# Attention block on one core: P.V of all sixteen heads in one block, in slot 3 of the following step

## The chip, the core and the metric

The kernel runs on one NeuronCore of a Trainium2 chip. Five engines work side by side, each through its own instruction stream in order: TensorE (PE, matrix products and transposes, results in PSUM), VectorE (DVE), ScalarE (ACT), GpSimd (POOL) and SyncE (SP, which issues most DMAs). They wait for one another through semaphores. The metric is the device time of one execution in microseconds; lower is better.

## What is computed

For each of sixteen batch elements of 256 tokens by 256 features: a layer norm scaled and shifted by a condition vector, sixteen-head attention with heads of 16 features, a projection, the residual sum and the same norm again.

```python
h = _sln(hidden, w, ln_g, ln_b, Wg, bg, Wb, bb)
qkv = (h @ Wqkv.T + bqkv).reshape(B, N, num_heads, hd, 3)
energy = jnp.einsum('bhqd,bhkd->bhqk', q, k)
att = jax.nn.softmax(energy, axis=-1) / D ** 0.5
out = jnp.einsum('bhqk,bhkd->bhqd', att, v)
out = jnp.moveaxis(out, 1, 2).reshape(B, N, D)
out = out @ Wp.T + bp
h1 = out + hidden
h2 = _sln(h1, w, ln_g, ln_b, Wg, bg, Wb, bb)
return h2 + h1
```

B = 16, N = D = 256, sixteen heads, everything float32.

## The kernel before

The program is a pipeline over batch elements. `step(b)`, written once for each engine, runs over sixteen **slots** h = 0 to 15, one for each head; after steps -1 to 14 a last step is written out by hand. Different batch elements are in different stages of one step:

- **Scores.** In slot h PE computes `scores(b, h)` into the banks `st` (two matmuls, keys by queries), and ACT turns them into exponentials `p32[:, h]` (L585). Banks `st0` and `st1` alternate, so scores of slot h wait for the exponential of slot h-2.
- **Maxima.** In the same slot PE computes `scores_max(b + 1, h)`, queries by keys, into the banks `sa` (two matmuls); DVE takes the row maxima `mx` from them (L664, `maximum`). These banks alternate too: `scores_max` of slot h waits for the maximum of slot h-2. After eight heads PE transposes the maxima (`transpose_max`, slots 1 and 9), ACT writes `m_h` and DVE `m_l` (`low_max`), which POOL sends by DMA into rows of the stacked queries, so that the exponentials need no subtraction.
- **Projections.** Q and K of b+2, V of b+1 and the output projection of b-1 come in quarters of three matmuls, in the slots that `Q_SLOTS`, `K_SLOTS`, `V_SLOTS` and `P_SLOTS` list.
- **P.V.** `weigh(b, g)` multiplies the exponentials of eight heads by V: 16 matmul instructions (32 rows of the trace), four of them side by side in column groups of 32, into bank `pv_ps[g]`. `PV_SLOTS = (10, 2)`: the first eight heads in slot 10 of step b, the other eight in slot 2 of step b+1. ACT copies a bank to `oT` (`evict_out`, L534), PE transposes it back (`out_by_token`, four transposes, L1034), DVE divides by the sums (`normalise`: `rec`, then `att`).
- **After both halves** PE transposes `att` (`turn_att`, slot 10, L1115), ACT copies the result to `aT_h` (L559), DVE subtracts for `aT_l` (`low_att`, L749), and the output projection takes both from slot 12 on. The quarter in slot 12 waits for `aT_l`.
- **The next input.** `turn_x(b + 3)` (four transposes) in slot 10, then `hT` and `hT_h` on ACT.

What DVE does between the maxima is the dictionary `between` of its `step`: (h, 0) stands before the maximum of slot h, (h, 1) behind it. `residual(b - 2, 0..5)` is the residual sum, its statistics and the two passes that write `y`; `norm1(b + 3, 0..2)` the statistics of the next input; `low_qk` the low parts of Q and K. Each engine keeps to its written order: an instruction that waits holds all that stands behind it on that engine.

Of the kernel before, what the change touches and what calls it, by code (L numbers as in the profile page):

```python
# [32 lines left out]
P = 128  # L33
B, N, D, H = 16, 256, 256, 16
HD = D // H
KT = D // P
# [17 lines left out]
S_O1, S_O0 = 3, 12  # L54
S_OT1, S_OT0 = 6, 14


def cond_block(nc, x, condT, vectors, WgT, WbT, WqkvT, WpT, bp, out):
    gb_dram = nc.dram_tensor("gb_rows", (B, 2 * D), F32, kind="Internal").ap()
    with ExitStack() as ctx:  # L60
# [10 lines left out]
        wqkv = sb("wqkv", [P, KT, 3 * D])  # L71
# [5 lines left out]
        wg = sb("wg", [P, KT, D])  # L77
# [36 lines left out]
        p32 = sb("p32", [P, H, KT * N])  # L114
# [138 lines left out]
        def max_sent(a, g):  # L253

            return 32 * (half(a) + (1 if g or par(a) else 0)) if a >= 0 else 0

# [223 lines left out]
        def _(act):  # L480
# [55 lines left out]
            def step(b):  # L536
                for h in range(H):
                    if h == S_O1:
                        evict_out(b - 1, 1)
                    if h == S_O0:  # L540
# [96 lines left out]
            for h in range(H):  # L637
                wait(act, st_done, 16 * (B - 1) + h + 1)
                if h % HH == 0:
                    wait(act, pv_done, 2 * (B - 2) + h // HH + 1)  # L640
                nc.scalar.activation(p32[:, h, :], last_st[h % 4][:], ACT.Exp).then_inc(exp_done, 1)
                if h == 1:
                    high_max(B - 1, 1, pv_ps[0])
# [12 lines left out]
        def _(dve):  # L656
# [169 lines left out]
            def step(b):  # L826


                between = {
                    (2, 1): [lambda: low_max(b, 1)],  # L830
                    (3, 0): [lambda: residual(b - 2, 0), lambda: residual(b - 2, 1)],
                    (4, 0): [lambda: residual(b - 2, 2), lambda: norm1(b + 3, 0)],
                    (4, 1): [lambda: residual(b - 2, 3), lambda: norm1(b + 3, 1)],
                    (5, 0): [lambda: norm1(b + 3, 2)],
                    (5, 1): [lambda: low_qk(b + 2, 0, m0, qh_ready, ql_ready)],
                    (7, 0): [lambda: normalise(b - 1, 1, 0)],
                    (7, 1): [lambda: low_qk(b + 2, 1, m1, kh_ready, kl_ready)],
                    (8, 0): [lambda: normalise(b - 1, 1, 1)],
                    (9, 1): [lambda: residual(b - 2, 4)],
                    (11, 0): [lambda: low_max(b + 1, 0), lambda: low_att(b - 1), lambda: residual(b - 2, 5)],  # L840
                    (15, 0): [lambda: normalise(b, 0, 0)],
                    (15, 1): [lambda: normalise(b, 0, 1)],
                }
                if first(b + 1):
                    for slot in ((4, 0), (4, 1), (5, 0), (5, 1), (7, 1), (11, 0)):
                        del between[slot]
# [96 lines left out]
        def _(pe):  # L943
# [63 lines left out]
            def weigh(b, g):  # L1007
# [11 lines left out]
                for q in range(2):  # L1019
                    for k in range(TT):  # L1020
                        for j in range(4):
                            h = HH * g + 4 * q + j
                            o = mm(pv_ps[g][32 * j:32 * j + VC, q * N:(q + 1) * N], v_st[:, p, k, h, :],
                                   p32[:, h, k * N:(k + 1) * N], k == 0, k == TT - 1)
# [110 lines left out]
            def last_weigh(half):  # L1135
# [7 lines left out]
                for k in range(TT):  # L1143
                    for j in range(4):
                        h = HH + 4 * half + j
                        o = mm(bank[32 * j:32 * j + VC, 0:N], v_st[:, p, k, h, :],
                               p32[:, h, k * N:(k + 1) * N], k == 0, k == TT - 1)
# [75 lines left out]
            def step(b):  # L1223
                for h in range(H):
# [11 lines left out]
                    for g in range(2):  # L1236
                        a = b - g
                        if h == PV_SLOTS[g] and has(a):
                            weigh(a, g)
                    if h == S_OT1:  # L1240
                        out_by_token(b - 1, 1)
                    if h == S_OT0:
                        out_by_token(b, 0)
                    if h == S_MT1 and has(b):
                        wait(pe, att_ready, 2 * (b - 1) + 1)
# [106 lines left out]
```

## Time and profile before

| | |
|---|---|
| median of 3 runs | 352.46 us (350.66 to 354.25) |
| the profiled execution, whole | 353.58 us |
| its span in the profile | 351.8 us |
| busy share of the span | PE 96%, DVE 85%, ACT 69%, POOL 45% |
| chain of work that ended last, by engine | PE 87%, DVE 5%, DMA 2% |
| clock granted to PE | 0.995 of full speed on average |

The profiled execution spent 1.8 us outside its span, and is 1.1 us above the median of the runs. In the rows below, a start to start distance is the time that an instruction holds its place in an engine's stream; the duration printed beside it reaches beyond that, since both matmuls and DVE operations overlap with the one behind.

### The profile page before, as it was taken

What the parts mean: (1) busy time and instruction counts of PE and PEld (TensorE: products, weight loads), DVE (VectorE), ACT (ScalarE), POOL (GpSimd) and SP (SyncE); (2) the same over time, 40 slices, a digit from 0 to 9 for tenths busy, and PEclk for the clock granted to TensorE, in tenths of its full rate; (3) what the DMA queues carried; (4) which work ended last, traced back from release to release, by engine and by line L of the source; (5) the groups of instructions that cost most, each with busy time, mean ns of one, the idle gap of its engine ahead of it and who ended that gap; (6) DMA issues with size and microseconds to landing.
All of it is one profiled execution on the core that took longest, in us unless ns stands there. A gap on an engine that the chain in (4) does not pass through costs nothing.

```text
span 351.8 us, 8975 instructions
## 1 busy us (share of the span) xinstructions
PE 336.8 (96%) x3170; PEld 290.8 (83%) x3171; DVE 299.9 (85%) x732; ACT 241.8 (69%) x472; POOL 156.7 (45%) x185
## 2 busy tenths in 40 slices
PE   7978899999999999999999999999999999999974
PEld 4757868889898888888898988888898988888753
DVE  4679677789898999989898989989898988998773
ACT  7643687767778686868678686868686786666730
POOL 5382271535464462726454553717354643234330
PEclk9999899999999999999999999999999999999999
DMA  8297344544546465555455455654556453642031
GB/s 240 73 229 195 84 122 123 154 132 125 169 133 158 137 179 154 146 160 144 138 154 158 134 159 150 171 161 133 164 140 157 103 159 104 174 124 63 4 89 60
DMA packets 47705, 48.87 MB, mean 139 GB/s; under 512 B 6287, under 2 KB 41374, under 8 KB 47662
## 3 DMA queue, kind: packets, MB, share of 16 engines
q1 hardware_dynamic: 44494, 46.74, 48.4%
q10 hardware_dynamic: 1184, 1.07, 1.1%
q0 software_dynamic: 1984, 0.51, 0.8%
q8 instruction: 25, 0.41, 0.5%
q14 instruction: 18, 0.15, 0.1%
HBM read 9.99 MB, written 4.23 MB: 40 GB/s over the span
## 4 chain that ended last, share of the span: by engine, by line
PE 87%; DVE 5%; DMA 2%; ACT 1%; issue 1%; ACTq 1%; POOL 0%; SPq 0%; DVEq 0%
PE m L945 25%; PE st L945 18%; PE sa L945 18%; PE pv L945 17%; PE pv L1034 4%; DVE mx L664 2%; PE pv L1115 2%; PE m L1074 2%; DMA kst<-qk_l 1%; DMA vrows<-vectors_dram 1%; DVE qk_l L699 1%; PE pv L1048 1%; ACTq L608 1%; DVE y L780 1%; PE m L1048 1%
## 5 line engine op out<-in xcount | busy, mean ns | idle before, releaser
L664 DVE TENSOR_REDUCE mx<-sa 128x2 f32<-128x512 f32 x256 | 171.8, 684 | 31.7 <-PE sa L945 30.7
L585 ACT ACTIVATE p<-st 128x512 f32<-128x512 f32 x240 | 141.0, 598 | 39.0 <-PE st L945 34.7
L945 PE MATMUL sa<-kst,qst 126*128 126x256 f32 x512 | 106.0, 289 | 3.1 <-DVE mx L664 2.0
L945 PE MATMUL st<-qst,kst 128*128 128x256 f32 x496 | 104.8, 294 | 0.5 <-DMA qst<-m_l 0.3
L945 PEld LDWEIGHTS st<-qst,kst 128*128 128x128 f32 x496 | 75.8, 190 | 14.2 <-issue 12.8
L945 PEld LDWEIGHTS sa<-kst,qst 126*128 126x128 f32 x512 | 79.2, 191 | 5.7 <-DVE mx L664 2.4
L365 POOL DMA_DIRECT2D qst<-m_h x31 | 17.6, 567 | 114.0 <-DVE m_l L673 114.0
L945 PE MATMUL pv<-p,v_st 128*32 128x256 f32 x1008 | 61.0, 382 | 0.0
L945 PEld LDWEIGHTS pv<-p,v_st 128*32 128x32 f32 x1008 | 29.5, 109 | 21.0 <-issue 1.4
L945 PE MATMUL m<-hT_h,wqkv_h 128*128 128x256 f32 x128 | 38.0, 311 | 1.6 <-POOL hT_l L406 0.9
L374 POOL TENSOR_SCALAR xn<-xa,mv,rstd 128x256 f32<-128x256 f32 x28 | 34.2, 1227 | 1.5
L945 PE MATMUL m<-hT_l,wqkv_h 128*128 128x256 f32 x128 | 34.5, 281 | 0.0
L945 PE MATMUL m<-hT_h,wqkv_l 128*128 128x256 f32 x128 | 34.5, 281 | 0.0
L420 POOL TENSOR_TENSOR rstd<-vare,minus_half 128x4 f32<-128x4 f32 (+1 forms) x16 | 14.9, 932 | 40.0 <-DVE vare L721 36.0
L534 ACT ACTIVATE oT<-pv 128x512 f32<-128x512 f32 x29 | 17.2, 594 | 21.6 <-PE pv L945 21.6
L699 DVE SCALAR_TENSOR_TENSOR qk_l<-m,vecs,qk_h 128x256 fp32r<-128x256 f32 x64 | 27.7, 475 | 1.1 <-ACT qk_h L506 1.0
L945 PEld LDWEIGHTS m<-hT_h,wqkv_h 128*128 128x128 f32 x128 | 24.4, 199 | 2.8 <-issue 1.7
L945 PEld LDWEIGHTS m<-hT_h,wqkv_l 128*128 128x128 f32 x128 | 23.8, 191 | 0.0
L945 PEld LDWEIGHTS m<-hT_l,wqkv_h 128*128 128x128 f32 x128 | 23.7, 191 | 0.0
L392 POOL TENSOR_TENSOR h1b<-h,gb 128x512 f32<-128x512 f32 x15 | 19.3, 1285 | 9.7 <-DMA gb<-gb_rows 9.7
L406 POOL TENSOR_TENSOR hT_l<-hT,hT_h 128x512 fp32r<-128x512 f32 x14 | 18.0, 1288 | 10.5 <-ACT hT_h L487 10.5
L383 POOL TENSOR_TENSOR xa<-xa,bias_b 128x512 f32<-128x512 f32 x16 | 20.6, 1291 | 0.0
(147 smaller groups left out, 566.0 us busy)
## 6 DMA issues: line engine op xcount, KB each, us to landing
qst<-qk_h SPq DMA_DIRECT2D x64, 128.0 KB, 2.4
qst<-qk_l SPq DMA_DIRECT2D x64, 128.0 KB, 2.5
kst<-qk_h SPq DMA_DIRECT2D x62, 128.0 KB, 2.5
kst<-qk_l SPq DMA_DIRECT2D x62, 128.0 KB, 2.7
xa<-x_dram SPq DMA_DIRECT2D x16, 256.0 KB, 3.0
gb<-gb_rows SPq DMA_DIRECT2D x16, 256.0 KB, 3.8
out_dram<-y SPq DMA_DIRECT2D x15, 256.0 KB, 2.2
wqkv<-WqkvT_dram SPq DMA_DIRECT2D x1, 512.0 KB, 5.6
```

The costliest lines, as they stand in the source:

```text
L365: pool.dma_start(raw(qst[MAX_ROW + r:MAX_ROW + 1 + r, p, g * HH:(g + 1) * HH, :]) .rearrange("a h (t n) -> a (h t) n", t=TT), raw(m[:, g, ...
L374: o = pool.tensor_scalar(xn[:, t, :], xbuf(a)[:, t, :], mv[:, t, 0:1], rstd[:, 0, t:t + 1], ALU.subtract, ALU.mult)
L383: pool.tensor_tensor(xbuf(a), xbuf(a), bias_b[:].rearrange("p (a n) -> p a n", a=1).broadcast_to([P, TT, D]), ALU.add).then_inc(xdb_ready, 1)
L392: pool.tensor_tensor(h1b[:], h1[:], gb[:, par(a), D:2 * D].rearrange("p (a n) -> p a n", a=1) .broadcast_to([P, TT, D]), ALU.add).then_inc ...
L406: pool.tensor_tensor(hT_l[:, par(a)], hT[:], hT_h[:, par(a)], ALU.subtract).then_inc(hTl_ready, 1)
L420: pool.tensor_tensor(rstd[:, which], vare[:, which], minus_half[:, which], ALU.pow).then_inc(rstd_ready, 1)
L534: nc.scalar.activation(oT[:, g, :], pv_ps[g][:], ACT.Copy).then_inc(oT_ready, 1)
L585: nc.scalar.activation(p32[:, h, :], st_ps[h % 2][:], ACT.Exp).then_inc(exp_done, 1)
L664: dve.tensor_reduce(mx[:, par(a), h // HH, (h % HH) * TT:(h % HH + 1) * TT], sa_ps[h % 2][:].rearrange("p (t n) -> p t n", t=TT), AX.X, AL ...
L699: o = dve.scalar_tensor_tensor(out=qk_l[:, par(a), t, g, :], in0=ps[:, g * N:(g + 1) * N], scalar=vecs[:, 4 + t, g:g + 1], in1=qk_h[:, par ...
L945: return nc.tensor.matmul(o, l, r, start=start, stop=stop)
L1034: o = nc.tensor.transpose(pv_ps[g][:, t * N + c * P:t * N + (c + 1) * P], oT[:, g, c * N + t * P:c * N + (t + 1) * P], ident[:])
```

## The change

Both calls of `weigh` for one batch element now stand behind one another in slot 3 of the following step. For that the exponentials of a whole step have to outlive it, so `p32` becomes a ring of twenty heads instead of sixteen (the weights `wqkv` and `wg`, which only the start reads, are laid into its last four). The two copies to `oT` stand together in slot 4 on ACT, the two `out_by_token` in slots 4 and 5 on PE, and `normalise` in slots 5 to 7 on DVE. Nearly all the work that DVE did between the maxima of slots 3 to 5 moves to one place before the maximum of slot 4. Some projection quarters shift by a slot or two; `turn_x` moves from slot 10 to 11, the copy of V on ACT from 9 to 10. Steps 1 to 14 have the joined block; in step 14 the first half of element 14 stays in slot 10, and the last step keeps its order.

```diff
-PV_SLOTS = (10, 2)
-
-Q_SLOTS, K_SLOTS, V_SLOTS, P_SLOTS = (0, 1, 3, 4), (4, 5, 5, 6), (7, 7, 8, 8), (12, 13, 14, 15)
-S_MT1, S_AT, S_MT0, S_XT = 1, 10, 9, 10
-S_QH, S_KH, S_VH = 5, 7, 9
+PV_SLOT, PV_LAST = 3, 10
+RING = 20
+
+Q_SLOTS, K_SLOTS, V_SLOTS, P_SLOTS = (0, 1, 1, 2), (4, 5, 6, 6), (7, 8, 8, 9), (12, 13, 14, 15)
+S_MT1, S_AT, S_MT0, S_XT = 1, 10, 9, 11
+S_QH, S_KH, S_VH = 4, 7, 10
...
-S_O1, S_O0 = 3, 12
-S_OT1, S_OT0 = 6, 14
+S_OUT, S_O0 = 4, 12
+S_OT, S_OT0 = (4, 5), 14
...
-        p32 = sb("p32", [P, H, KT * N])
+        p32 = sb("p32", [P, RING, KT * N])
...
+                    if h == S_OUT:
+                        evict_out(b - 1, 0)
+                        evict_out(b - 1, 1)
...
-                        if h % HH == 0:
+                        if h % HH == RING - H:
                             wait(act, pv_done, 2 * (b - 1) + h // HH + 1)
-                        nc.scalar.activation(p32[:, h, :], st_ps[h % 2][:], ACT.Exp).then_inc(exp_done, 1)
+                        nc.scalar.activation(p32[:, ring(b, h), :], st_ps[h % 2][:], ACT.Exp).then_inc(exp_done, 1)
...
-                    wait(pe, ml_ready, 2 * b + 2)
+                    wait(pe, ml_ready, 2 * (b + 1 if b < B - 2 else b) + 2)
...
-                    for g in range(2):
-                        a = b - g
-                        if h == PV_SLOTS[g] and has(a):
-                            weigh(a, g)
-                    if h == S_OT1:
-                        out_by_token(b - 1, 1)
-                    if h == S_OT0:
+                    if h == PV_SLOT and has(b - 1):
+                        weigh(b - 1, 0)
+                        weigh(b - 1, 1)
+                    if h in S_OT:
+                        out_by_token(b - 1, S_OT.index(h))
+                    if h == PV_LAST and b == B - 2:
+                        weigh(b, 0)
+                    if h == S_OT0 and b == B - 2:
                         out_by_token(b, 0)
```

Where the order changes most, in a step of the middle. On PE, slots 10 to 12 before (`xn` is the next input, `att` the attention output by token, `wp` the output projection's weights):

```order
L945 MATMUL sa<-kst,qst 128x256 [waits max_done]
L945 MATMUL sa<-kst,qst 128x256
L1074 MATMUL m<-ident,xn 128x128 [waits xn_ready,v_ready]
L1074 MATMUL m<-ident,xn 128x128 x3
L1115 MATMUL pv<-ident,att 128x128 [waits att_ready]
L1115 MATMUL pv<-ident,att 128x128 x3
L945 MATMUL pv<-p,v_st 32x256 [waits v_ready,ml_ready,att_ready,exp_done]
L945 MATMUL pv<-p,v_st 32x256 x15
L945 MATMUL st<-qst,kst 128x256 [waits exp_done]
```

The same place on PE in the changed kernel, from the transposes of `att` to the first quarter of the output projection:

```order
L1121 MATMUL pv<-ident,att 128x128 [waits att_ready]
L1121 MATMUL pv<-ident,att 128x128 x3
L951 MATMUL st<-qst,kst 128x256 [waits exp_done]
L951 MATMUL st<-qst,kst 128x256
L951 MATMUL sa<-kst,qst 128x256 [waits max_done]
L951 MATMUL sa<-kst,qst 128x256
L1080 MATMUL m<-ident,xn 128x128 [waits xn_ready,v_ready]
L1080 MATMUL m<-ident,xn 128x128 x3
L951 MATMUL st<-qst,kst 128x256 [waits exp_done]
L951 MATMUL st<-qst,kst 128x256
L951 MATMUL sa<-kst,qst 128x256 [waits max_done]
L951 MATMUL sa<-kst,qst 128x256
```

The block of P.V has gone from between the transposes of `att` and the pairs behind them; the transposes of `xn` stand there instead, one slot later than before. On PE, the new place of the block, from the maxima's pair of slot 3 to the scores of slot 4:

```order
L951 MATMUL sa<-kst,qst 128x256 [waits max_done]
L951 MATMUL sa<-kst,qst 128x256
L951 MATMUL pv<-p,v_st 32x256 [waits v_ready,ml_ready,att_ready,exp_done]
L951 MATMUL pv<-p,v_st 32x256 x15
L951 MATMUL pv<-p,v_st 32x256 [waits aTl_ready,att_ready,exp_done]
L951 MATMUL pv<-p,v_st 32x256 x15
L951 MATMUL st<-qst,kst 128x256 [waits exp_done]
```

Its first matmul waits for `ml_ready`, the `m_l` of the maxima that were transposed in slot 1 of the same step; the block that stood in slot 2 before did not. On DVE, around slot 11 in the changed kernel, where the list is as it was before (`y` is the output, `aT_l` feeds the output projection):

```order
L786 SCALAR_TENSOR_TENSOR y<-h,mv,gb 128x256 [waits gb_in0,y_out0]
L786 SCALAR_TENSOR_TENSOR y<-h,mv,gb 128x256
L670 TENSOR_REDUCE mx<-sa 128x2 [waits mT_done,sa_done]
L679 SCALAR_TENSOR_TENSOR m_l<-m,m_h 16x128 [waits mh_ready]
L755 TENSOR_TENSOR aT_l<-pv,aT_h 128x512 [waits aTh_ready]
L794 SCALAR_TENSOR_TENSOR y<-y,rstd,h1b 128x256 [waits h1b_ready,rstd_ready,ln2_step]
L794 SCALAR_TENSOR_TENSOR y<-y,rstd,h1b 128x256
L670 TENSOR_REDUCE mx<-sa 128x2 [waits mT_done,sa_done] x8
```

These rows keep their order and their places between the maxima; what PE does beside them is different.

## Rows read from the trace of the kernel before

**Rows 1.** Timeline of PE: first scores of steps 2 and 12 (start and duration in us)
```profile
73.75 0.28 PE L945 MATMUL st<-qst,kst 128*128 128x256 f32 x1
...
268.73 0.28 PE L945 MATMUL st<-qst,kst 128*128 128x256 f32 x1
```
**Rows 2.** Busy time in step 6: stretch, length, PE, PEld, DVE, ACT, POOL; clock
```profile
151.75:171.24 19.49, 19.49 (x196) 17.29 (x195) 17.84 (x45) 14.57 (x30) 9.37 (x10) 1.00 0.52 151
```
**Rows 3.** Timeline of PE around the block in slot 2 of step 7
```profile
172.54 0.28 PE L1048 MATMUL pv<-ident,mx 128*128 128x128 f32 x1
...
173.24 0.40 PE L945 MATMUL sa<-kst,qst 126*128 126x256 f32 x2
173.56 1.93 PE L945 MATMUL pv<-p,v_st 128*32 128x256 f32 x32
175.43 0.51 PE L945 MATMUL st<-qst,kst 128*128 128x256 f32 x2
175.77 0.40 PE L945 MATMUL sa<-kst,qst 126*128 126x256 f32 x2
176.01 0.28 PE L945 MATMUL m<-hT_h,wqkv_h 128*128 128x256 f32 x1
```
**Rows 4.** The same for slots 10 to 13 of step 6
```profile
163.69 0.51 PE L945 MATMUL sa<-kst,qst 126*128 126x256 f32 x2
164.03 0.60 PE L1074 MATMUL m<-ident,xn 128*128 128x128 f32 x4
164.47 0.60 PE L1115 MATMUL pv<-ident,att 128*128 128x128 f32 x4
165.00 1.93 PE L945 MATMUL pv<-p,v_st 128*32 128x256 f32 x32
...
167.92 0.28 PE L945 MATMUL m<-wp_h,aT_h 128*128 128x256 f32 x1
...
168.27 0.39 PE L945 MATMUL st<-qst,kst 128*128 128x256 f32 x2
...
168.74 0.28 PE L945 MATMUL m<-wp_h,aT_h 128*128 128x256 f32 x1
```
**Rows 5.** The same, a narrow window: the last four matmuls of that block
```profile
166.54 0.40 PE L945 MATMUL pv<-p,v_st 128*32 128x256 f32 x4
```
**Rows 6.** Timeline of DVE, slots 7 to 11 of step 6 (in brackets: idle before)
```profile
161.85 0.86 DVE L699 SCALAR_TENSOR_TENSOR qk_l<-m,vecs,qk_h 128x256 fp32r<-128x256 f32 x2
162.62 0.41 DVE L687 TENSOR_TENSOR att<-pv,rec 128x256 f32<-128x256 f32 x1
162.96 1.28 DVE L664 TENSOR_REDUCE mx<-sa 128x2 f32<-128x512 f32 x2
164.15 0.87 DVE L780 SCALAR_TENSOR_TENSOR y<-h,mv,gb 128x256 f32<-128x256 f32 x2
164.94 0.68 DVE L664 TENSOR_REDUCE mx<-sa 128x2 f32<-128x512 f32 x1
165.54 0.27 DVE L673 SCALAR_TENSOR_TENSOR m_l<-m,m_h 16x128 fp32r<-16x128 f32 x1
165.74 0.69 DVE L749 TENSOR_TENSOR aT_l<-pv,aT_h 128x512 fp32r<-128x512 f32 x1
166.35 0.87 DVE L788 SCALAR_TENSOR_TENSOR y<-y,rstd,h1b 128x256 f32<-128x256 f32 x2
167.65 0.69 DVE L664 TENSOR_REDUCE mx<-sa 128x2 f32<-128x512 f32 x1 [0.42 <-PE sa L945]
```
**Rows 7.** Timeline of DVE, slot 2 of step 7
```profile
173.67 0.69 DVE L664 TENSOR_REDUCE mx<-sa 128x2 f32<-128x512 f32 x1 [0.24 <-PE sa L945]
```
**Rows 8.** Timeline of ACT, slot 11 of step 6
```profile
165.11 0.60 ACT L559 ACTIVATE aT_h<-pv 128x512 fp32r<-128x512 f32 x1 [0.34 <-PE pv L1115]
165.60 1.02 ACT L568 ACTIVATE hT<-m,bfull,gfull 128x256 f32<-128x256 f32 x2
166.65 0.63 ACT L487 ACTIVATE hT_h<-hT 128x512 fp32r<-128x512 f32 x1
```

More of the change, by code:

```diff
@@ L76, in cond_block @@
         wp_l = sb("wp_l", [P, KT, D], F32R)
-        wg = sb("wg", [P, KT, D])
         wb = sb("wb", [P, KT, D])
@@ L113, in cond_block @@
         m_l = sb("m_l", [HH * TT, 2, P], F32R)
-        p32 = sb("p32", [P, H, KT * N])
+        p32 = sb("p32", [P, RING, KT * N])
+        wqkv = p32[:, H:H + 3, :].rearrange("p a n -> p (a n)").rearrange("p (k n) -> p k n", k=KT)
+        wg = p32[:, H + 3, :].rearrange("p (k n) -> p k n", k=KT)
         oT = sb("oT", [P, 2, 2 * N])
@@ L255, in max_sent, with ring @@
             return 32 * (half(a) + (1 if g or par(a) else 0)) if a >= 0 else 0
+        def ring(a, h):
+            return (H * a + h) % RING
         def xbuf(a):
@@ L537, in step @@
                 for h in range(H):
-                    if h == S_O1:
-                        evict_out(b - 1, 1)
-                    if h == S_O0:
+                    if h == S_O0 and b == B - 2:
                         evict_out(b, 0)
@@ L638, in _ @@
                 wait(act, st_done, 16 * (B - 1) + h + 1)
-                if h % HH == 0:
+                if h % HH == RING - H:
                     wait(act, pv_done, 2 * (B - 2) + h // HH + 1)
-                nc.scalar.activation(p32[:, h, :], last_st[h % 4][:], ACT.Exp).then_inc(exp_done, 1)
+                nc.scalar.activation(p32[:, ring(B - 1, h), :], last_st[h % 4][:], ACT.Exp).then_inc(exp_done, 1)
                 if h == 1:
@@ L830, in step @@
                     (2, 1): [lambda: low_max(b, 1)],
[L831 to L836, printed above, removed]
+                    (4, 0): [lambda: residual(b - 2, 0), lambda: residual(b - 2, 1), lambda: residual(b - 2, 2),
+                             lambda: norm1(b + 3, 0), lambda: residual(b - 2, 3), lambda: norm1(b + 3, 1),
+                             lambda: norm1(b + 3, 2), lambda: low_qk(b + 2, 0, m0, qh_ready, ql_ready)],
+                    (5, 0): [lambda: normalise(b - 1, 0, 0)],
+                    (5, 1): [lambda: normalise(b - 1, 0, 1)],
+                    (6, 0): [lambda: normalise(b - 1, 1, 0)],
+                    (7, 0): [lambda: normalise(b - 1, 1, 1)],
                     (7, 1): [lambda: low_qk(b + 2, 1, m1, kh_ready, kl_ready)],
-                    (8, 0): [lambda: normalise(b - 1, 1, 1)],
                     (9, 1): [lambda: residual(b - 2, 4)],
                     (11, 0): [lambda: low_max(b + 1, 0), lambda: low_att(b - 1), lambda: residual(b - 2, 5)],
-                    (15, 0): [lambda: normalise(b, 0, 0)],
-                    (15, 1): [lambda: normalise(b, 0, 1)],
-                }
+                }
+                if b == B - 2:
+                    between[(15, 0)] = [lambda: normalise(b, 0, 0)]
+                    between[(15, 1)] = [lambda: normalise(b, 0, 1)]
                 if first(b + 1):
-                    for slot in ((4, 0), (4, 1), (5, 0), (5, 1), (7, 1), (11, 0)):
-                        del between[slot]
+                    between = {}
                     between[(2, 0)] = [lambda: low_qk(1, 0, m0, qh_ready, ql_ready)]
@@ L1023, in weigh @@
                             o = mm(pv_ps[g][32 * j:32 * j + VC, q * N:(q + 1) * N], v_st[:, p, k, h, :],
-                                   p32[:, h, k * N:(k + 1) * N], k == 0, k == TT - 1)
+                                   p32[:, ring(b, h), k * N:(k + 1) * N], k == 0, k == TT - 1)
                 o.then_inc(pv_done, 1)
@@ L1146, in last_weigh @@
                         o = mm(bank[32 * j:32 * j + VC, 0:N], v_st[:, p, k, h, :],
-                               p32[:, h, k * N:(k + 1) * N], k == 0, k == TT - 1)
+                               p32[:, ring(B - 1, h), k * N:(k + 1) * N], k == 0, k == TT - 1)
                 o.then_inc(pvt_done, 1)
@@ L1235, in step @@
                         turn_att(b - 1)
-                    for g in range(2):
-                        a = b - g
-                        if h == PV_SLOTS[g] and has(a):
-                            weigh(a, g)
-                    if h == S_OT1:
-                        out_by_token(b - 1, 1)
-                    if h == S_OT0:
+                    if h == PV_SLOT and has(b - 1):
[6 more added lines that the diff above has]
+                    if h == S_OT0 and b == B - 2:
                         out_by_token(b, 0)
                     if h == S_MT1 and has(b):
-                        wait(pe, att_ready, 2 * (b - 1) + 1)
+                        wait(pe, att_ready, 2 * (b - 2) + 1)
                         if first(b):
```

1 line of the change is left out of this document (removed).

## The prediction

> **What bounds the kernel now.** I read first how regular the steps are, then which engine is busy all through one, then the rows around the two blocks. The first scores of steps 2 and 12 start at 73.75 and 268.73 [rows 1], ten steps apart, so one step is 19.50 us. In such a step PE is busy for 19.49 of 19.49 us and DVE for 17.84 [rows 2]: PE sets the pace, and DVE has only 1.65 us to spare. Its places between the maxima matter, because PE computes maxima for two heads at most ahead of DVE. That limit shows already in one place: the maxima of slot 10 start at 163.69, just after the maximum of slot 8 ended (162.96 + 0.68 = 163.64), and hold PE for 0.34 instead of 0.24 us [rows 4, 6]. So a semaphore from DVE takes 0.05 us to reach PE, and a wait costs 0.10 us beyond its length.
>
> What keeps DVE from holding PE up elsewhere is the block in slot 10. DVE's group at slot 11 (`m_l`, `aT_l` and the second pass of `y`, ending 0.79 after 166.35) fits beside PE's block from 165.00 to 166.87, and DVE then even waits 0.42 us for the next maxima [rows 4, 6]. The same block covers the way from the transposes of `att` over `aT_h` and `aT_l` to the output projection's first quarter: `aT_l` ends at 166.43, and the quarter starts at 167.92 [rows 4, 6].
>
> **What the change saves on PE.** Going into the block costs 0.08 us (the pair before it holds 0.32 instead of 0.24), leaving it 0.10 (0.34 instead of 0.24), and the block itself holds 1.87 us [rows 3]. Inside, eight groups of four matmuls start from 165.00 to 166.54 [rows 4, 5], 1.54 / 7 = 0.22 us apart, so eight more groups in the same block cost about 1.75, not 1.87. One block fewer saves 0.08 + 0.10 + 0.12 = 0.30 us a step. The wait of slot 10 goes too, another 0.10: in the count further down the maximum of slot 8 ends at 0.43 + 0.60 + 0.77 + 0.69 = 2.49, and PE comes to slot 10's maxima at 2.93. Were there no other wait, a step would take 19.50 - 0.40 = 19.10 us.
>
> The Trainium skill says in TensorEngine Tiling (Array Packing), Key Properties, that changing the tiling mode drains TensorE, and P.V is the only work here in columns of 32. The trace agrees: it shows the 0.08 and 0.10 us above. By this rule alone the change gains, and that is the first rival below.
>
> **What it costs in slot 3.** The block's first matmul now waits for `m_l` of maxima transposed in slot 1. Counted from that transpose: it takes 0.11 (172.54 to 173.24 is 0.70, less a quarter, 0.35, and half a pair, 0.24 [rows 3, 4]); then two quarters (0.70), the pair of slot 2 (0.47), a quarter (0.35), the pair of slot 3 (0.47) and the way in (0.08) bring PE to 2.18. The pair is 168.27 to 168.74, the quarter 167.92 to 168.27 [rows 4]. DVE must first take the maximum of slot 2. Those maxima start at 0.11 + 0.70 + 0.24 = 1.05 on PE; the maximum follows 0.43 later (173.24 to 173.67 [rows 3, 7]), at 1.48; `m_l` follows 0.60 behind it and lasts 0.27 [rows 6], to 2.35; PE sees it at 2.40. That is a wait of 0.22 us, with everything behind it on PE held.
>
> DVE's long list before the maximum of slot 4 costs nothing: it lies in a stretch in which PE, busy with P.V for 3.6 us, delivers no maxima. The copies to `oT` also stand beside the block: the first half is copied during the second, and the second while PE does slot 4.
>
> **What it costs in slots 11 to 13.** The list at slot 11 stays, but the block beside it is gone. I count from the start of slot 7's maxima on PE. Ahead of slot 13's maxima PE has: the rest of that pair 0.24 and a quarter 0.35; slot 8, pair and two quarters, 1.17; slot 9, pair, transpose, quarter, 0.93; slots 10 and 11, a pair and four transposes each (0.47 + 0.44, the latter 164.03 to 164.47 [rows 4]), 1.82; slot 12, pair and quarter, 0.82; half a pair 0.24. Sum 5.57 us.
>
> DVE in the same stretch, by start to start distances [rows 6]: 0.43 to the maximum of slot 7, which takes 0.60; low part of K 0.77; maxima of slots 8 and 9 1.19; first pass of `y` 0.79; maximum of slot 10 0.60; `m_l` 0.20; `aT_l` 0.61; second pass of `y` 0.79; maximum of slot 11 in full 0.69. With the semaphore's 0.05 that is 6.72. All these stand in this order, and none waits for PE by more than 0.03, since PE is ahead. So slot 13's maxima come 6.72 - 5.57 = 1.15 us late, plus 0.10. About 0.34 of it shows earlier, at the output projection's first quarter: `aT_l` ends at 0.43 + 0.60 + 0.77 + 1.19 + 0.79 + 0.60 + 0.20 + 0.69 = 5.27, and PE sees it at 5.32; PE is there at 5.57 - 0.35 - 0.24 = 4.98.
>
> DVE cannot make this up ahead of slot 7: its lag there starts from zero, as it waits for PE's maxima after the block (the pairs of slots 4 to 7 are 1.2 us or so apart, a maximum takes 0.60).
>
> A step then takes 19.10 + 0.22 + 1.15 + 0.10 = 20.57 us, 1.07 more than before.
>
> **Is ScalarE any help?** No, it would hold PE at almost the same place. From the transposes of `att` (164.47) to the copy `aT_h` (165.11) 0.64; the copy 0.49; an exponential taken as the same 0.49; `hT` 1.05 (165.60 to 166.65); `hT_h` at least 0.5, then the exponential of slot 12, 0.6 [rows 4, 8]: 3.8 us. PE waits for it at the scores of slot 14, which it would reach 0.44 + 0.91 + 0.82 + 0.82 = 2.99 after those transposes. So even if DVE were fast, PE would lose about 0.8 us there. In step 1, which has no `y` on DVE, this takes DVE's place.
>
> **The ends.** Step 0 loses its block and four transposes: 1.87 + 0.18 + 0.44 = 2.5 at most, nothing at least; ScalarE's group is then uncovered there too, and I take 1.3. Steps 1 to 12: 12 x 1.07 = 12.8. Step 13 has no `turn_x`, so PE was 0.44 faster there and is now held to DVE's time all the same: 1.07 + 0.44 = 1.5. Step 14 takes the half that step 0 lost without its own way in, 1.75, and the wait of slot 3, more with no Q quarters ahead of it, 0.4: 2.1. The last step is as before. Sum: -1.3 + 12.8 + 1.5 + 2.1 = 15.1 us. The profiled execution, on which this rests, took 353.58; it would become 368.7. It was 1.1 us above the median, so against 352.46 I expect 367.5 us.
>
> **Rivals.**
> - *The saving alone.* By the rule of the drain: 13 steps x -0.40, step 0 -1.3, step 14 +1.75, in all -4.8: 347.7 us. It speaks for it that DVE has 1.65 us to spare over a step, against it that the spare time lies in the wrong slots: it decides if slot 11's list were done 1.15 us sooner than the rows add up to. 4%.
> - *Only the chains, not the list.* If just the wait of slot 3 (0.22) and of the output projection (0.34 + 0.10) stayed, a step would be 19.76, 0.26 more: 13 x 0.26 - 1.3 + 2.1 = +4.2, 356.6, and with the shortest of both waits within 1%. Against it stands that `y` is written ahead of slot 11's maximum. 5%.
> - *More waits than I count.* Queries and keys for the next maxima are sent by SP when slot 7's scores and the low part of K are done; if their landing held the next step's slot 0 by another 0.5 us, 13 x 0.5 brings 374. DVE's chain moves the step's end back as well, which gives them room. 6%.
> - The forecast: 85%.
>
> **How the numbers follow.** A measurement of this kernel tells about 1% from no change, 348.9 to 356.0. The range must hold errors of the count: half of the loss of slots 11 to 13 would give 367.5 - 13 x 0.55 = 360.3; another 0.4 us a step 372.7. So 360.5 to 373, which leaves out the first two rivals and the top of the third. Faster 0.04; same 0.04 (the lower part of the second rival, the upper of the first); slower 0.92.
>
> **What would show it right or wrong.** In the profile after, a step of 20.5 to 20.6 us; one block of 3.6 us a step; PE idle or late before the block in slot 3 (0.2, for `m_l`), at the output projection's first quarter (0.3, for `aT_l`), and before slot 13's maxima (0.8, for the maximum of slot 11); DVE without idle time from slot 7 to slot 12, and idle after the block instead. Wrong would be a step under 19.5, DVE with idle time between slots 8 and 11, or a wait at the start of slot 0.

## The result, and the profile after

The changed kernel takes 368.24 us (median of 4 runs, 367.39 to 370.46) where the kernel before took 352.57 (4 runs, 350.66 to 354.25): a ratio of 1.046, 95% interval 1.041 to 1.051. The forecast was 367.5, range 360.5 to 373. The profiled execution took 367.54 us, with a span of 365.7.

In that profile PE is busy for 92% of the span (96% before), DVE for 84% (85%), ACT for 65% (69%).

The timeline of PE gives the first scores of steps 2 and 12 (start and duration), which answers [rows 1]:

```profile
71.45 0.28 PE L951 MATMUL st<-qst,kst 128*128 128x256 f32 x1
...
276.87 0.28 PE L951 MATMUL st<-qst,kst 128*128 128x256 f32 x1
```

The windows view of step 6 answers [rows 2] (stretch, length, busy time and count of PE, PEld, DVE, ACT, POOL; granted clock):

```profile
153.61:174.15 20.54, 19.59 (x197) 17.76 (x195) 18.38 (x45) 14.43 (x30) 9.35 (x11) 1.00 0.53 145
```

Ten steps in 205.42 us: a step is 20.54 us instead of 19.50. PE was busy all through a step before; now 0.95 us of each step is idle. PE does the same matmuls, so the loss is waiting. The timeline of PE in step 6 shows where (start, duration, line, operation, count; in brackets the idle time before, and what ended it). First slot 3, then slots 12 and 13:

```profile
156.77 0.40 PE L951 MATMUL sa<-kst,qst 126*128 126x256 f32 x2
157.41 3.66 PE L951 MATMUL pv<-p,v_st 128*32 128x256 f32 x64 [0.24 <-DVE m_l L679]
161.00 0.51 PE L951 MATMUL st<-qst,kst 128*128 128x256 f32 x2
...
169.85 0.41 PE L951 MATMUL sa<-kst,qst 126*128 126x256 f32 x2
170.43 0.39 PE L951 MATMUL m<-wp_h,aT_h 128*128 128x256 f32 x1 [0.17 <-DVE aT_l L755]
...
170.89 0.39 PE L951 MATMUL st<-qst,kst 128*128 128x256 f32 x2
171.82 0.50 PE L951 MATMUL sa<-kst,qst 126*128 126x256 f32 x2 [0.54 <-DVE mx L670]
172.16 0.28 PE L951 MATMUL m<-wp_h,aT_h 128*128 128x256 f32 x1
```

Three places are held, all by DVE. The idle time in brackets is less than what is lost, because a modelled matmul end covers part of it; starts tell the loss. The pair before the block holds 0.64 us (156.77 to 157.41) instead of the 0.32 of [rows 3]: 0.32 lost. The pair before the output projection's first quarter holds 0.58 instead of 0.24, and the quarter itself 0.46 (170.43 to 170.89) instead of the 0.35 of [rows 4]: 0.45 lost. The scores of slot 13 hold 0.93 (170.89 to 171.82) and the maxima behind them 0.34, each instead of 0.24: 0.79 lost. In all 1.56 us, and 20.54 - 1.56 = 18.98 us is the step without waits. The block itself holds 3.59 us.

The other side is the timeline of DVE in the same step, which answers [rows 6 and 7]:

```profile
156.38 0.69 DVE L670 TENSOR_REDUCE mx<-sa 128x2 f32<-128x512 f32 x1 [0.59 <-PE sa L951]
156.99 0.27 DVE L679 SCALAR_TENSOR_TENSOR m_l<-pv,m_h 16x128 fp32r<-16x128 f32 x1
...
165.51 0.69 DVE L670 TENSOR_REDUCE mx<-sa 128x2 f32<-128x512 f32 x1 [0.17 <-PE sa L951]
166.12 0.86 DVE L705 SCALAR_TENSOR_TENSOR qk_l<-m,vecs,qk_h 128x256 fp32r<-128x256 f32 x2
166.91 1.29 DVE L670 TENSOR_REDUCE mx<-sa 128x2 f32<-128x512 f32 x2
168.12 0.87 DVE L786 SCALAR_TENSOR_TENSOR y<-h,mv,gb 128x256 f32<-128x256 f32 x2
168.91 0.68 DVE L670 TENSOR_REDUCE mx<-sa 128x2 f32<-128x512 f32 x1
169.51 0.27 DVE L679 SCALAR_TENSOR_TENSOR m_l<-m,m_h 16x128 fp32r<-16x128 f32 x1
169.70 0.67 DVE L755 TENSOR_TENSOR aT_l<-pv,aT_h 128x512 fp32r<-128x512 f32 x1
170.30 0.86 DVE L794 SCALAR_TENSOR_TENSOR y<-y,rstd,h1b 128x256 f32<-128x256 f32 x2
```

`m_l` ends at 157.26, and the block's first group of matmuls starts at 157.41. From 165.51 on no row has idle time ahead of it: DVE works its list through, and PE, which had the block to do beside it before, stands behind it. In [rows 6] DVE was the one that waited after the second pass of `y`, for 0.42 us.

ScalarE's group around slot 12, from its timeline, answers [rows 8] (`aT_h` starts at 168.94, ahead of these rows):

```profile
169.90 1.05 ACT L574 ACTIVATE hT<-m,bfull,gfull 128x256 f32<-128x256 f32 x2
170.98 0.63 ACT L492 ACTIVATE hT_h<-hT 128x512 fp32r<-128x512 f32 x1
171.51 1.07 ACT L591 ACTIVATE p<-st 128x512 f32<-128x512 f32 x2
```

The exponential of slot 12 starts only at 171.51, yet PE shows no wait for ScalarE: in slot 13 it waits for DVE until 171.82 anyway. Over the whole run the waits view lists (us in total, times, longest):

```profile
...
PE sa L951 <- DVE mx L670: 9.9, 18, 1.2
...
PE pv L951 <- DVE m_l L679: 3.7, 14, 0.5
...
PE m L951 <- DVE aT_l L755: 2.2, 12, 0.3
```

The times of the first scores of every step in both traces give the whole difference of the spans, in us:

| stretch | before | after | difference | forecast |
|---|---|---|---|---|
| to the first scores of step 0 | 35.59 | 33.09 | -2.5 | 0 |
| step 0 | 18.67 | 17.28 | -1.4 | -1.3 |
| step 1 | 19.49 | 21.08 | +1.6 | +1.07 |
| steps 2 to 11 | 10 x 19.50 | 10 x 20.54 | +10.4 | +10.7 |
| step 12 | 19.50 | 20.79 | +1.3 | +1.07 |
| step 13 | 19.03 | 20.69 | +1.7 | +1.5 |
| step 14 | 17.07 | 19.37 | +2.3 | +2.1 |
| last step | 27.44 | 28.02 | +0.6 | 0 |
| sum | 351.77 | 365.73 | +14.0 | +15.1 |

### The profile page after: what moved, and what is told of

Read it like the earlier page. It is cut to its first block, busy times and chain, and to the rows that moved or that the text cites. A ratio compares the mean times of both kernels' runs of the same rounds, so it can differ in the third digit from the quotient of the medians.

```text
span 365.7 us, 8975 instructions
## 1 busy us (share of the span) xinstructions
PE 335.7 (92%) x3171; PEld 294.7 (81%) x3171; DVE 306.8 (84%) x732; ACT 239.4 (65%) x472; POOL 157.8 (43%) x185
## 3 DMA queue, kind: packets, MB, share of 16 engines
q10 hardware_dynamic: 1184, 1.07, 1.1%
## 4 chain that ended last, share of the span: by engine, by line
PE 60%; DVE 21%; issue 10%; ACT 4%; DMA 2%; ACTq 1%; POOL 1%; DVEq 0%
PE pv L951 16%; PE m L951 15%; PE sa L951 12%; PE st L951 11%; DVE mx L670 9%; PE pv L1040 4%; DVE y L786 3%; DVE qk_l L705 3%; DVE y L794 2%; DVE m_l L679 1%; ACT qst L595 1%; DMA kst<-qk_l 1%; DMA qst<-m_l 1%; ACT p L591 1%; ACT hT L574 1%
## 5 line engine op out<-in xcount | busy, mean ns | idle before, releaser
L951 PE MATMUL st<-qst,kst 128*128 128x256 f32 x496 | 103.2, 290 | 2.2 <-ACT p L591 2.1
L951 PEld LDWEIGHTS sa<-kst,qst 126*128 126x128 f32 x512 | 78.3, 189 | 15.9 <-DVE mx L670 12.7
L951 PE MATMUL pv<-p,v_st 128*32 128x256 f32 x1008 | 58.1, 380 | 3.7 <-DVE m_l L679 3.7
L951 PEld LDWEIGHTS pv<-p,v_st 128*32 128x32 f32 x1008 | 36.6, 110 | 20.0 <-issue 5.6
L951 PEld LDWEIGHTS m<-hT_h,wqkv_h 128*128 128x128 f32 x128 | 23.5, 189 | 3.5 <-issue 1.2
L411 POOL TENSOR_TENSOR hT_l<-hT,hT_h 128x512 fp32r<-128x512 f32 x14 | 17.9, 1280 | 15.1 <-ACT hT_h L492 15.1
L951 PE MATMUL m<-wp_h,aT_h 128*128 128x256 f32 x64 | 20.0, 313 | 2.3 <-DVE aT_l L755 2.2
```

The costliest lines, as they stand in the source:

```text
L411: pool.tensor_tensor(hT_l[:, par(a)], hT[:], hT_h[:, par(a)], ALU.subtract).then_inc(hTl_ready, 1)
L951: return nc.tensor.matmul(o, l, r, start=start, stop=stop)
```

## The experiments

A step below is the distance from one step's first scores to the next's, in the steps of the middle of the profiled execution. "Beside" gives the kernel before on the same chip. The theory is that of the prediction: three holds by DVE and, hidden behind them, one by ScalarE. The rivals are that PE itself is slower with the joined block, or that one hold alone carries the loss and the others only move.

**The wait for `m_l` alone.** `m_l` is written before the maximum of slot 2 instead of after it:

```diff
-                    (2, 1): [lambda: low_max(b, 1)],
+                    (2, 0): [lambda: low_max(b, 1)],
```

> The changed kernel, with m_l of the second eight heads made before the maximum of slot 2 instead of behind it; nothing else. A step of the changed kernel takes 20.54 us, and the block in slot 3 starts 0.24 us late for m_l. If that wait is a loss of its own, as the prediction counted it, it goes and a step takes 20.25 to 20.35 us, with the waits in slots 12 and 13 as they were. If the joined block starves VectorE (the rival theory: the idle time behind the block is the loss), an earlier block changes nothing: 20.5 us.

Measured: a step of 20.25 us, 0.29 less than 20.54; the run took 364.83 us, beside 351.13. The wait before the block is gone, and those of slots 12 and 13 are as they were (idle 0.17 and 0.53). So the hold of slot 3 is a loss of its own, and what is given back there isn't taken again further on.

**ScalarE's group alone.** One half of `hT` is written in slot 12, the other in slot 13, `hT_h` in slot 14 (in short):

```diff
-                        for k in range(KT):
+                        for k in range(KT if first(b + 1) else 1):
...
+                    if h == S_XT + 2 and not first(b + 1) and has(b + 3):
+                        nc.scalar.activation(hT[:, 1, :], ...).then_inc(hT_ready, 1)
-                    if h == (X_FIRST if first(b + 1) else S_XT) + 1:
+                    if h == (X_FIRST + 1 if first(b + 1) else S_XT + 3):
                         high_h(b + 3)
```

> The changed kernel, with ScalarE's hT of the next input spread over slots 12 and 13 and hT_h moved to slot 14, so that its exponentials of slots 12 to 14 come sooner; VectorE as it was. The theory of the prediction: VectorE's list still holds PE, 20.5 to 20.6 us a step. If ScalarE's group were the holder: about 20.0 us.

Measured: 20.55 us, 368.69, beside 351.13. No change: ScalarE holds nothing that DVE doesn't hold as long.

**Both passes of `y` out of slots 9 and 11, a first try.** The second pass goes to slot 14, among the last maxima (in short):

```diff
...
                              lambda: norm1(b + 3, 2), lambda: low_qk(b + 2, 0, m0, qh_ready, ql_ready),
+                             lambda: residual(b - 2, 4)],
...
-                    (9, 1): [lambda: residual(b - 2, 4)],
-                    (11, 0): [lambda: low_max(b + 1, 0), lambda: low_att(b - 1), lambda: residual(b - 2, 5)],
+                    (11, 0): [lambda: low_max(b + 1, 0), lambda: low_att(b - 1)],
+                    (14, 0): [lambda: residual(b - 2, 5)],
```

> The changed kernel, with VectorE's two passes of y moved: the first from slot 9 to the end of the list beside the block, the second from slot 11 to slot 14. The theory of the prediction: the wait of slot 13's maxima (0.7 us) goes, but ScalarE's group (aT_h, hT, hT_h) then holds PE at the scores of slot 14 by about 0.5, so a step falls only to about 20.3 us. Rival one, VectorE's list is the only cause: 19.5 to 19.7 us. Rival two, the block itself is the cause: 20.5 us.

Measured: 21.67 us in the steps that run the second pass, 1.13 more instead of 0.24 less; 380.6 us, beside 351.13. Step 2 took 20.32: its slot 0 lies ahead of the first second pass, which starts at 91.6 us. The timelines of POOL, DVE and PE show why:

```profile
199.57 1.27 POOL L411 TENSOR_TENSOR hT_l<-hT,hT_h 128x512 fp32r<-128x512 f32 x1 [0.98 <-ACT hT_h L492]
199.95 2.60 DVE L794 SCALAR_TENSOR_TENSOR y<-y,rstd,h1b 128x256 f32<-128x256 f32 x2
200.81 1.46 POOL L388 TENSOR_TENSOR xa<-xa,bias_b 128x512 f32<-128x512 f32 x1
```

```profile
181.64 0.47 PE L952 MATMUL sa<-kst,qst 126*128 126x256 f32 x2 [1.13 <-DVE mx L670]
```

The two operations of the second pass take 2.60 us; in the kernel before one takes 0.48 in the median and 0.56 at most. They lie beside two operations of POOL, and end at 202.55, 0.28 us after the second of these (202.27). The next maxima then come late, and PE stands 1.13 us in slot 0 of the next step (the second row, one step earlier).

**Is it POOL?** The same kernel with POOL's sum of the bias moved from slot 0 to slot 4, so that only `hT_l` lies beside the second pass:

```diff
-                    if h == 0 and has(b - 1):
+                    if h == 4 and has(b - 1):
                         add_bias(b - 1)
```

> The run with y moved to slots 4 and 14 (21.67 us a step, second pass of y 1.17 and 1.51 us), with one thing more: GpSimd's bias sum goes from the start of the step to behind the maxima rows of slot 3, so that only hT_l still runs beside the second pass of y. If an operation of VectorE on two operands in SBUF waits for GpSimd's tensor operation beside it, the first of the two still takes about 1.2 us and the second 0.48 again, and a step falls by about 1.0 to 20.6 us. If slot 14 is simply a bad place: 1.17 and 1.51 as before, 21.7 us.

Measured: 20.63 us, 366.85, beside 350.71. Timelines of POOL and DVE:

```profile
192.29 1.27 POOL L411 TENSOR_TENSOR hT_l<-hT,hT_h 128x512 fp32r<-128x512 f32 x1 [0.98 <-ACT hT_h L492]
```

```profile
192.68 1.56 DVE L794 SCALAR_TENSOR_TENSOR y<-y,rstd,h1b 128x256 f32<-128x256 f32 x2
```

The second operation, now clear of POOL, takes 0.47 (1.51 before), the first, still beside `hT_l`, 1.16: its end at 193.84 is again 0.28 after POOL's (193.56). So it is POOL's operation that holds DVE's, and the miss of the run before is explained by where I had put `y`, not by the theory of slots 11 to 13.

**Both of these together** (`y` as in the first try and ScalarE's group spread):

> Both: y moved as in the second kernel and hT spread as in the third. The theory of the prediction, two holders at nearly the same place, either of which is enough: the two together bring far more than the sum of each alone, a step of 19.9 us (left: 0.24 at slot 3, 0.2 to 0.3 at the output projection's first quarter). If the two effects simply add up: about 20.3 us. If the block itself is the cause: 20.5 us.

Measured: 20.2 us in most steps (19.87 to 20.49), 361.85, beside 351.13. `hT_l` comes later here, and `y` starts ahead of it and takes 0.48 as before; now POOL's `hT_l` takes 1.58 instead of 1.27, and the next step's first quarter of Q waits 0.2 us for it. Better than either alone, but muddied by POOL; hence the next two.

**`y` in a place where POOL doesn't work.** Both passes go into the long list of slot 4, the second one step later (in short; SP sends the output a step later too):

```diff
...
-                    (4, 0): [lambda: residual(b - 2, 0), lambda: residual(b - 2, 1), lambda: residual(b - 2, 2),
-                             lambda: norm1(b + 3, 0), lambda: residual(b - 2, 3), lambda: norm1(b + 3, 1),
+                    (4, 0): [lambda: residual(b - 3, 5),
+                             lambda: residual(b - 2, 0), lambda: residual(b - 2, 1), lambda: residual(b - 2, 2),
+                             lambda: norm1(b + 3, 0), lambda: residual(b - 2, 3), lambda: residual(b - 2, 4),
+                             lambda: norm1(b + 3, 1),
...
-                    (9, 1): [lambda: residual(b - 2, 4)],
-                    (11, 0): [lambda: low_max(b + 1, 0), lambda: low_att(b - 1), lambda: residual(b - 2, 5)],
+                    (11, 0): [lambda: low_max(b + 1, 0), lambda: low_att(b - 1)],
```

> In the run with y moved the second pass of y took 1.17 and 1.51 us an operation instead of 0.48, while GpSimd ran hT_l and the bias sum beside it, and the step became 21.67 us. Here both passes of y stand in VectorE's list beside the block of slot 3 (the second pass of the element before at its front, the first pass behind the statistics), where GpSimd has no tensor work; ScalarE is as in the changed kernel. If GpSimd beside it was the cause, the second pass takes 0.87 us for its two operations again, slot 13's maxima no longer wait, and ScalarE's group holds PE at slot 14's scores by about 0.5: a step of 20.3 us. If moving y is itself at fault: 21 us or more. If VectorE's list was the only holder: 19.5 to 19.7 us.

Measured: 20.30 us, 363.38, beside 353.19. The timeline of PE, at slot 14:

```profile
190.57 0.28 PE L954 MATMUL m<-wp_h,aT_h 128*128 128x256 f32 x1
...
191.45 0.51 PE L954 MATMUL st<-qst,kst 128*128 128x256 f32 x2 [0.36 <-ACT p L592]
```

DVE holds slot 13 no more. PE now stands in slot 14, for ScalarE: the quarter ahead of the scores holds 0.88 us (190.57 to 191.45) instead of 0.35, and the scores 0.34 (the maxima start at 191.79) instead of 0.24, so 0.63 is lost here. With 1.6 us of DVE's work taken out of slots 9 and 11, the step gets only 0.24 shorter.

**The same, and ScalarE's group spread:**

> The same, with ScalarE's hT spread over slots 12 and 13 and hT_h in slot 14. hT spread alone brought nothing (20.55 us). The theory of two holders: 19.8 us a step, with 0.24 left at slot 3 and 0.2 to 0.3 at the output projection's first quarter. If effects only add: 20.3 us.

Measured: 19.89 us in most steps, 360.44, beside 353.19. So of DVE's list and ScalarE's group, `y` alone gives back 0.24, ScalarE alone 0.0, both 0.65. In this run PE's only idle time of a usual step is the 0.22 before the block, for `m_l`; but by its starts such a step (91.91 to 111.81) also loses 0.36 at the output projection's first quarter, for `aT_l`, and 0.22 at Q's first quarter, for POOL's `hT_l`. With the 0.30 at the block that is 0.88, and 19.89 - 0.88 = 19.01 us is again the step without waits.

**What is a wait that comes just too late worth?** The kernel before, with one division moved behind the maximum of slot 8:

```diff
-                    (8, 0): [lambda: normalise(b - 1, 1, 1)],
+                    (9, 0): [lambda: normalise(b - 1, 1, 1)],
```

> The kernel before with one line moved: the second half's division by the sums (att) from before the maximum of slot 8 to before that of slot 9. The prediction read that slot 10's maxima wait 0.01 us for the maximum of slot 8 and lose 0.10 because of it. If so, a step falls from 19.50 to 19.40 us and the time by about 1.2 us. If such a short wait costs only its length: 19.49 us, no change.

Measured: a step of 19.39 us instead of 19.50; 350.83 us (median of 6 runs, 348.82 to 351.22) against 353.19 (11 runs), a ratio of 0.9925 (0.990 to 0.995): the only version whose time lies below the kernel before. The steps give some 1.3 of the 2.4 us between the medians. The first scores of step 0 start at 33.46 us in its profile and at 35.59 in the kernel before, and that start varies from one execution to the next (below); so the step shows what the wait is worth, not the ratio. The timeline of PE, slot 10:

```profile
161.07 0.40 PE L945 MATMUL sa<-kst,qst 126*128 126x256 f32 x2
161.31 0.60 PE L1074 MATMUL m<-ident,xn 128*128 128x128 f32 x4
```

The maxima of slot 10 hold 0.24 us; in [rows 4] they held 0.34. A wait that can hardly be seen cost 0.10 us, and the saving of that wait, which the prediction counted beside the block's, is real.

**What does a block cost?** That kernel, with the block of slot 2 cut in two, four heads in slot 2 and four in slot 3:

```diff
-                            weigh(a, g)
+                            weigh(a, g, (0, 1) if g == 0 else (0,))
+                    if h == PV_SLOTS[1] + 1 and has(b - 1):
+                        weigh(b - 1, 1, (1,))
```

> The kernel before with att moved (19.39 us a step, PE without a wait), and its block of slot 2 cut in two: four heads in slot 2, four in slot 3, so that a step has three blocks of P.V instead of two with the same matmuls. The prediction priced one block at 0.30 us beyond its matmuls (0.08 in, 0.10 out, 0.12 at its ends). If so, a step takes 19.68 to 19.73 us and the time rises by about 4.5 us. If blocks cost nothing by themselves: 19.4 us.

Measured: 19.71 us, 0.32 more for one block more; 356.75 us (4 runs) against 352.54 (7 runs), ratio 1.010 (1.006 to 1.015). The timeline of PE around a half block:

```profile
194.26 0.40 PE L945 MATMUL sa<-kst,qst 126*128 126x256 f32 x2
194.59 1.07 PE L945 MATMUL pv<-p,v_st 128*32 128x256 f32 x16
195.59 0.50 PE L945 MATMUL st<-qst,kst 128*128 128x256 f32 x2
```

The half holds 1.00 us, so two halves hold 0.13 more than the whole of 1.87 in [rows 3]; the way in (0.33 instead of 0.24) and out (0.34) are paid once more.

**All holds removed.** `m_l` early, `aT_l` one maximum later, and the quarters of Q and of the output projection moved so that the first of each starts a slot later:

```diff
-Q_SLOTS, K_SLOTS, V_SLOTS, P_SLOTS = (0, 1, 1, 2), (4, 5, 6, 6), (7, 8, 8, 9), (12, 13, 14, 15)
+Q_SLOTS, K_SLOTS, V_SLOTS, P_SLOTS = (1, 1, 2, 2), (4, 5, 6, 6), (7, 8, 8, 9), (13, 13, 14, 15)
...
-                    (2, 1): [lambda: low_max(b, 1)],
+                    (2, 0): [lambda: low_max(b, 1)],
...
+                    (11, 0): [lambda: low_max(b + 1, 0)],
+                    (11, 1): [lambda: low_att(b - 1)],
```

This starts from the kernel with both passes of `y` in slot 4 and ScalarE's group spread.

> The same, with the two waits that are left taken away as well: m_l before the maximum of slot 2, the output projection's first quarter in slot 13 with aT_l behind the maximum of slot 11, Q's quarters in slots 1 and 2. By the prediction's count PE's own work is 19.1 us a step; with some shorter waits that remain 19.2 to 19.4 us, about the 19.50 of the kernel before or a little less: 350 to 353 us. If the joined block costs something by itself, more than 19.6 us a step.

Measured: 19.48 us in most steps, 354.9 us (median of 6 runs) against 353.19 (11 runs), ratio 1.006 (1.003 to 1.008). Some steps are longer, up to 20.59. The windows view of a usual step, the timeline of PE in its slots 6 and 13, and the timeline of PE where a long step ends:

```profile
108.23:127.71 19.48, 19.48 (x196) 17.45 (x195) 17.87 (x45) 13.97 (x30) 9.35 (x11) 1.00 0.54 149
```

```profile
117.98 0.40 PE L960 MATMUL st<-qst,kst 128*128 128x256 f32 x2
118.33 0.50 PE L960 MATMUL sa<-kst,qst 126*128 126x256 f32 x2
118.67 0.28 PE L960 MATMUL m<-hT_h,wqkv_h 128*128 128x256 f32 x1
...
124.64 0.50 PE L960 MATMUL st<-qst,kst 128*128 128x256 f32 x2
124.98 0.40 PE L960 MATMUL sa<-kst,qst 126*128 126x256 f32 x2
125.26 0.38 PE L960 MATMUL m<-wp_h,aT_h 128*128 128x256 f32 x1
125.48 0.28 PE L960 MATMUL m<-wp_h,aT_l 128*128 128x256 f32 x1
```

```profile
148.30 0.51 PE L960 MATMUL st<-qst,kst 128*128 128x256 f32 x2 [0.94 <-DMA qst<-m_l]
```

The 1.04 us that the change costs in a step are won back, but of the 0.5 that it saves on PE only 0.02 shows. The usual step has no idle time on PE, yet three short holds: slot 6's pair takes 0.69 us instead of 0.47, slot 13's pair 0.62 instead of 0.47, and the first matmul of the quarter behind it 0.22 instead of 0.12. That is 0.47 in all, and 19.48 - 0.47 = 19.01 us is the step without them. By the timelines slot 6 waits for DVE's maximum of slot 4, which ends at 118.27 behind the long list, the scores of slot 13 for ScalarE's exponential of slot 11 (to 124.59), and the quarter for `aT_l` (to 125.21). Two of the long steps (20.59 and 20.48) end in a wait for the transfer of `m_l` into the queries of the next step; a third (20.17) loses more time in slot 6, and some in slot 0 to the low part of K.

**Is what is left PE's or DVE's?** The same kernel with the second half of the block moved back to a slot of its own:

```diff
                         weigh(b - 1, 0)
+                    if h == PV_SLOT + 1 and has(b - 1):
                         weigh(b - 1, 1)
```

> The changed kernel with all its waits taken away (19.48 us in most steps), and its joined block split again, the first half in slot 3 and the second in slot 4. If PE's own work is what bounds that kernel now, the second block costs its 0.30: about 19.8 us a step. If VectorE bounds it, less than half of that shows: 19.5 to 19.6.

Measured: 19.56 us in most steps, 0.08 more; 357.33, beside 352.54. An additional block that costs 0.32 us in the kernel before costs 0.08 here. So three quarters of a block's price is hidden in this version: PE's own time doesn't set its step alone. By the timeline of PE the 0.22 of slot 6 is gone here, since with the second block PE comes to slot 6 later, and the holds of slot 13 are as they were. That the step would fall to 19.0 us without these holds was not tried by a run of its own.

## Why the prediction came out

**The saving, 0.40 us: right in kind, 0.1 too small.** The step without its waits is 18.98 us by the rows of the changed kernel, 19.01 in each of two versions of the experiments, and 19.10 in the prediction. Two parts were measured apart: 0.11 for the wait of slot 10 (19.50 to 19.39), 0.32 for a block (19.39 to 19.71), counted as 0.10 and 0.30. A third, which I did not count, is a short hold of the kernel before at the scores of slot 14: they take 0.29 us there (169.09 to 169.38 in step 6) instead of 0.23. The count of the joined block (1.87 + 1.75 = 3.62) stands against 3.59.

**The wait for `m_l`, 0.22 and 0.10: the 0.10 was left out.** 0.32 by the rows, 0.29 when it is taken away. The prediction's sum has the 0.22 alone there, since I had not added the 0.10 of a wait at this place: `m_l` ends at 157.26 and the block starts 0.15 later, not 0.05.

**Slots 11 to 13, 1.15 and 0.10: right in place, kind and size.** Measured 0.45 at the output projection's first quarter, of which 0.34 ahead of it, as counted, and 0.79 in slot 13: 1.24 in all against 1.25. By the sum 19.10 + 0.22 + 1.25 = 20.57; measured 18.98 + 0.32 + 1.24 = 20.54. That the step is right to 0.03 is luck: the saving counted 0.1 too small and the 0.10 forgotten at the block cancelled.

**ScalarE as a second holder: right.** The prediction said that with a fast DVE PE would still lose about 0.8 at slot 14. With `y` out of the way the scores of slot 14 came 0.53 late and held 0.10 longer, and 0.36 was lost ahead of them for `aT_l` in slot 12: 0.89 of lateness where the sum said 0.8. And neither engine's share could be won back without the other's.

**Step 1: half a microsecond short.** I counted 1.07 for it, and it lost 1.6. The timeline of PE at its start, and at its end:

```profile
51.15 0.50 PE L951 MATMUL sa<-kst,qst 126*128 126x256 f32 x2 [0.31 <-DVE mx L670]
...
69.68 0.51 PE L951 MATMUL st<-qst,kst 128*128 128x256 f32 x2 [0.37 <-ACT p L591]
```

The maxima of its slot 0 are late: they start 0.78 us after the first scores, not 0.24. The weight load waits there 0.5 us for the transfer of the low part of K. SP issued it 2.4 us ahead of step 1's first scores (47.98 to 50.37), in the kernel before 5.2 us ahead: step 0 was 1.4 us shorter, and an issue of SP ahead of it took 1.74 us instead of 0.60. (The row puts the wait down to DVE's maximum; by the weight load's wait it is the transfer.) That is the third rival's mechanism, once and not in every step. At the step's end it is ScalarE that holds slot 14, as forecast for a step without `y`.

**The ends.** Step 13 and step 14 came within 0.2 us of their terms. Step 12 was 0.25 longer than the steps ahead of it, since the weight load of the next scores waited 0.3 us for the transfer of `m_l`. Step 0, -1.4 against the -1.3 that I took, is no confirmation. The windows view of step 0 in the kernel before, in the changed kernel, and in the first try with `y`, whose step 0 has the same work as the changed kernel's (columns as in the windows above, the clock being the third number from the end):

```profile
35.59:54.25 18.66, 17.14 (x132) 14.56 (x131) 13.43 (x30) 13.19 (x27) 9.27 (x10) 0.91 0.34 94
```

```profile
33.09:50.37 17.28, 13.38 (x97) 11.68 (x95) 13.49 (x29) 12.26 (x26) 8.47 (x10) 1.00 0.37 99
```

```profile
33.62:52.43 18.81, 14.91 (x97) 13.22 (x95) 13.51 (x29) 12.39 (x26) 8.47 (x10) 0.91 0.35 93
```

In each of the three PE stood idle for 0.93 us near the start of the step, waiting for `hT_l`. Behind that the granted clock fell to 0.50 for some 3 us in the first and the third, and stayed at 1.00 in the second. With the clock down, the joined kernel's step 0 takes as long as that of the kernel before. The clock fell there in all three profiles with the old order and in three of ten with the joined block; why is open, and so is what the work taken out of step 0 is worth by itself.

The last step was counted at nothing and lost 0.6. The windows view of a stretch of its output projection, first after, then before:

```profile
357.00:358.20 1.20, 1.20 (x6) 1.20 (x7) 0.19 (x1) 0.00 (x0) 0.00 (x0) 0.50 0.58 218
```

```profile
343.70:345.10 1.40, 1.40 (x9) 1.34 (x10) 0.78 (x2) 0.00 (x0) 0.00 (x0) 1.00 0.50 187
```

PE had stood idle for 1.98 us (2.06 before) and then worked for about 1.6. The granted clock was 0.50, 1.2 GHz, over the stretch behind that in the changed kernel, and 1.00 in the kernel before. It is the same work on the same path, so this is not the change's doing; why the clock fell in one and not in the other is open.

**The start.** The first scores came 2.5 us earlier in the profile of after. Over the 13 profiles of this study they come at 33.1 to 33.9 us in nine and at 35.1 to 35.6 in four, the kernel before being one of these four; kernels with the same first instructions fall on both sides. So this too varies from one execution to the next. The single execution thus gained 2.5 at the start and 1.4 in step 0, where the clock stayed up, and lost 0.6 at the end. With such differences between executions the sum of the whole cannot be checked to better than about 2 us: that the forecast lies 0.7 us from the median measured is in part luck. What bears the prediction out is the length of the steps from 2 to 11 and the place of their holds.

**The rivals.** The saving alone (347.7) is refuted by every hold; its premise, DVE's 1.65 us to spare, lay in the wrong slots, as said. Only the chains (356.6) is refuted by slot 13. What the block covers was worth more than the 0.32 us that it costs. The Trainium skill's rule that a change of the tiling mode drains TensorE (TensorEngine Tiling (Array Packing), Key Properties) would fit the 0.09 on the way into a block and the 0.10 on the way out, but these don't show it: four transposes, which keep the 128*128 mode, also have a first matmul behind them that holds 0.20 instead of 0.12 (161.94 to 162.14 in step 6).

**What I got wrong on the way** is the first try with `y`. I expected 20.3 and measured 21.67, since I had priced a pass of `y` at 0.8 us wherever it stands.

## What to carry to other kernels

A block of work on the bounding engine is also the cover for what other engines do beside it: before joining or moving one, list what lies beside it, and count both sides from a common start to the next point where one waits for the other. Here joining saves 0.5 us a step and uncovers 1.56. When two engines end their lists nearly together, taking away one shows next to nothing (0.24 and 0.0, where both give 0.65), so test them together before calling either harmless. And look for waits that are just met too late: one of them cost 0.10 us a step, and moving a single division in the kernel before was enough to win it back.

## What was new of the hardware

**An operation of DVE on operands in SBUF can be held by POOL.** The second pass of `y` reads two tensors in SBUF. Over the run of the first try, the source view gives (shortest, median and longest in ns) the first line, for the kernel before the second:

```profile
L794 DVE SCALAR_TENSOR_TENSOR y<-y,rstd,h1b x30: 473/1178/1511, 91.6 to 369.2; 128x256 f32<-128x256 f32 x30
```

```profile
L788 DVE SCALAR_TENSOR_TENSOR y<-y,rstd,h1b x30: 461/477/560, 88.3 to 342.8; 128x256 f32<-128x256 f32 x30
```

Beside a tensor operation of POOL that had started first it took 1.17 and 1.51 us instead of 0.48, and each time ended 0.28 us after POOL's. The maxima, which read PSUM, kept their 0.6 to 0.68 beside POOL. When `y` had started first it was POOL's operation that grew, from 1.27 to 1.58. The Trainium skill states this in SBUF — State Buffer, "SBUF: two separate sides": when a VectorE operation with two SBUF inputs meets a GpSimd operation that reads SBUF, the one that starts first keeps the pair of ports that both share until its instruction ends, and the other is blocked. The runs agree, with these numbers; the prediction had no use for it, since the change moved no such operation beside one of POOL.

**Small transfers can land late.** In the version with all holds removed, scores waited four times for the 8 KB of `m_l`, 1.2 us at most; in the kernel before and in the changed kernel once each, 0.5 and 0.3. In the long step that ends at 148.30, POOL sent them at 144.25 us, and SP sent the output at 144.39 right behind. That these larger transfers delay the small ones is likely, but was not tried.
